# DPP attention stage: own-key products, value weights and the mask of the found places on GpSimd; values held for four tiles

## The chip, the core and the metric
The kernel runs on one core of a Trainium2 chip as one program. The core has five engines that each take instructions in their own order: PE (TensorE, matmuls), DVE (VectorE), ACT (ScalarE), POOL (GpSimd) and SP, which here only issues DMAs. They meet at semaphores alone. The metric is the device time of one execution in microseconds (us), and lower is better. Times below are of the profiled execution unless said otherwise.

## What is computed
Six layers follow one another on x of shape 32 x 16 x 16 x 192: a mamba layer, a Fourier layer, the attention of this case (`l2a`), a gated mixture of experts, a memory attention and a second mixture. The change touches the attention alone. It works on 32 images of 256 tokens (two tiles of 128), with 12 heads of 16 channels. For each query token it finds the 8 most similar earlier keys, forms all pairs and triples of the token itself with one or two of them, scores each by the log-determinant of its Gram matrix, and mixes the softmax outputs of these sets by the probabilities of the scores:

```python
sim = k @ q_i
sim = jnp.where(jnp.arange(Tn) <= i, sim, -jnp.inf)
_, top_idx = jax.lax.top_k(sim, M)                      # M = 8
...
for comb in COMBS:                                      # one or two of the 8 slots
    valid = slot_valid[slots].all(axis=1) & ~slot_is_i[slots].any(axis=1)
    idx = jnp.concatenate([jnp.full((nc, 1), i), top_idx[slots]], axis=1)
    K = k[idx]; V = v[idx]
    gram = jnp.einsum('cnd,cmd->cnm', K, K)
    log_det = jnp.log(jnp.where(valid, jnp.linalg.det(gram), 1.0) + 1e-06)
    w = jax.nn.softmax(jnp.einsum('cnd,d->cn', K, q_i) / HS ** 0.5, axis=1)
    out_s = jnp.einsum('cn,cnd->cd', w, V)
...
probs = jax.nn.softmax(scores / TEMP)
y_soft = probs @ outs
...
return y @ W_proj.T + b_proj
```

Places with an index of the token itself or later are void; that is the mask.

## The kernel before
`dpp_attention_phase` writes out one program per engine. An image has six steps `i` = 0 to 5 (STEPS). In a step the find works on four of the twelve heads (QUAD = 4) of one tile: `t = i // 3`, so steps 0 to 2 are tile 0, with 128 keys, and steps 3 to 5 tile 1, with 256. `steps` unrolls the first and the last image and runs the other 30 in a loop of two images; `back(lag)` names the step that lies `lag` steps behind, so each engine works on several steps at once. `q` counts steps, `r = n * 2 + t` counts tiles.

The path of one step's four heads:
- PE `scores` writes similarities into PSUM, one step ahead. DVE `find` takes four MAX8 (L2485) and four FIND_INDEX8 (L2489) from it, then masks with two small operations (L2498 into `gone`, L2501 into `idxm`).
- PE `turn_indices` turns `idxm` (L2622), ACT copies it to `idxT` (L2269), SP writes it to DRAM and reads it back spread over all partitions (`spread`).
- One step later DVE `compare` makes the one-hot (L2534) and PE `gather` fetches keys and values with it (L2660, 96 matmuls for tile 0, 192 for tile 1, into three PSUM buffers `g`). ACT copies them out to `keys` and `values` (L2261 to L2263).
- Two steps later DVE `products` multiplies keys with keys (L2514, L2516) and keys with the token's own key (L2519) into `prod`, and `sums` reduces all of it to `dots` (L2526).

The work for a whole tile follows at fixed lags behind its last step: `det_stage` (lag 3, in steps 2 and 5), `log_stage` (lag 4, steps 0 and 3), `weigh_stage` (lag 5, steps 1 and 4) and `add_out` (lag 6, steps 2 and 5). `weigh_stage` ends with the value weights: L2461 multiplies `values` with `alpha` into `pv`. In the same step PE `turn_output` sums and turns `pv` (L2632, 36 matmuls) into PSUM `m`, and ACT `turned` copies it to `yT` (L2241). In the next step PE `project` (L2642) runs right behind the scores, and DVE `add_out` (L2473) adds its result to `x_res` ahead of `compare`.

PE also computes the next image's projections in seven units (`front`), three in step 1 and two each in steps 2 and 3. POOL squares and splits the keys, 32 times four large operations, released by `prod_ready`, which DVE sets right before its reduction. Per step DVE's order is `find`, the tile stage, `add_out`, `compare`, `products`, `det_end`, `sums`; PE's is `turn_indices`, `scores`, `project`, `front`, `turn_output`, `gather`.

## Time and profile before

| | us |
|---|---|
| median of 3 runs | 6926.5 (6921.05 to 6927.41) |
| profiled execution | 6929.71 |
| its span, first to last instruction | 6928.0 |
| DVE busy in the span | 4586.2 |
| PE busy | 4892.4 |
| ACT busy | 2648.7 |
| POOL busy | 1447.6 |

The attention stage runs from about 1500 to 4590 us. In the page's slices one digit is a fortieth of the span, 173 us, in tenths of busy time. In a timeline a row gives start, duration, engine, line, operation and tiles; in square brackets stands the idle time before it and what ended it. A row with "x4" merges four instructions. The end of a matmul is modelled, so PE's durations are less sure than DVE's. L numbers of this section and of the rows are lines of the kernel before; in the changed kernel the same code stands up to 47 lines lower down.

### The profile page before, as it was taken

The numbers are of one execution on the slowest core, as the hardware profiler recorded it, in microseconds if no ns is written. First come the engines' busy times: TensorE is split into PE (matmuls) and PEld (weight loads), VectorE is DVE, ScalarE is ACT, GpSimd is POOL, SyncE is SP. The second block draws the span as 40 slices with busy tenths as digits, with TensorE's granted clock in tenths as the row PEclk, the third lists the DMA queues.
The fourth block names the chain that finished last, engine by engine and source line by source line (L and its number), as shares of the span: only waits on it lengthen the run. The fifth ranks groups of instructions, "written<-read, shape, count | busy, mean of one in ns | idle before, by whom it ended". The sixth has DMA issues, their size and how long they took to land. (4 is left out here: it accounts for less than half of the span.)

```text
span 6928.0 us, 139785 instructions
## 1 busy us (share of the span) xinstructions
PE 4892.4 (71%) x46024; PEld 3814.4 (55%) x46025; DVE 4586.2 (66%) x10128; ACT 2648.7 (38%) x8929; POOL 1447.6 (21%) x1237
## 2 busy tenths in 40 slices
PE   6777777967777777777777777751794397169990
PEld 2333335756656666666666566551583376169990
DVE  5777773249999999999999999952464444212223
ACT  3334332225555455554554555532220132223330
POOL 2332331110000000000000000005325300554447
PEclk8777778977676777667776676655897697589995
DMA  4000000011111111111111111111222102111113
GB/s 139 7 5 7 7 0 6 0 38 69 69 65 68 69 69 69 69 69 67 69 72 63 69 69 69 69 39 53 72 76 72 41 0 60 51 53 46 45 42 109
DMA packets 139932, 369.61 MB, mean 53 GB/s; under 512 B 29410, under 2 KB 94667, under 8 KB 113716
## 3 DMA queue, kind: packets, MB, share of 16 engines
q1 hardware_dynamic: 105556, 283.58, 11.8%
q0 software_dynamic: 33792, 78.69, 3.6%
q8 instruction: 313, 5.13, 0.3%
q14 instruction: 271, 2.22, 0.1%
HBM read 286.69 MB, written 75.50 MB: 52 GB/s over the span
## 5 line engine op out<-in xcount | busy, mean ns | idle before, releaser
L2660 PE MATMUL l2a_g<-l2a_feat,l2a_onehot 128*128 128x33 bf16 x27648 | 780.9, 183 | 403.7 <-ACT l2a_values L2263 202.1
L2660 PEld LDWEIGHTS l2a_g<-l2a_feat,l2a_onehot 128*128 128x128 bf16 x27648 | 765.3, 100 | 473.6 <-issue 237.3
L2526 DVE TENSOR_REDUCE l2a_dots<-l2a_prod 128x144 f32<-128x2304 f32 x192 | 489.6, 2550 | 4.5
L2609 PE MATMUL l2a_s<-l2a_qkT 32*128 32x128 f32 (+1 forms) x1536 | 486.1, 452 | 0.0
L1892 PE MATMUL l_y<-l_hc,l_selT 128*96 128x512 f32 x384 | 300.2, 876 | 262.2 <-POOL l_hc L1730 261.7
L2632 PE MATMUL l2a_m<-main_ident,l2a_pv 128*96 128x128 f32 x2304 | 335.2, 317 | 152.2 <-DVEq L2467 152.2
L2632 PEld LDWEIGHTS l2a_m<-main_ident,l2a_pv 128*96 128x96 f32 x2304 | 327.2, 199 | 172.3 <-issue 168.8
L1730 POOL TENSOR_TENSOR l_hc<-l_hs,l_bc 128x512 f32<-128x512 f32 x192 | 243.4, 1268 | 717.3 <-DVE l_hs L1797 716.1
L2534 DVE TENSOR_SCALAR l2a_onehot<-l2a_spread,l2a_pos 128x4096 bf16<-128x4096 bf16 x288 | 360.7, 1281 | 43.8 <-DVE l2a_hd L2428 20.1
L2609 PEld LDWEIGHTS l2a_s<-l2a_qkT 32*128 32x128 f32 x1536 | 310.6, 250 | 85.6 <-issue 37.9
L700 PE MATMUL l3f_expert_h<-l3f_tT,l3f_w_own 96*128 96x256 f32 x2592 | 333.6, 287 | 8.9 <-POOL l3f_w_own L657 6.7
L2514 DVE TENSOR_TENSOR l2a_prod<-l2a_keys 128x1536 f32<-128x1536 f32 x192 | 336.1, 1750 | 0.2 <-DVE l2a_pv L2465 0.2
L2304 POOL TENSOR_TENSOR l2a_rest_f<-l2a_feat 128x384 f32<-128x384 f32 x32 | 26.4, 826 | 1456.2 <-ACT l2a_feat L2173 1456.2
L764 DVE TENSOR_TENSOR l3f_tT<-l3f_expert_tp,l3f_tT 96x512 fp32r<-96x512 f32 x72 | 49.5, 687 | 421.5 <-ACT l3f_tT L731 421.5
L740 ACT ACTIVATE l3f_hT<-l3f_expert_h,l3f_b 128x256 f32<-128x256 f32 x432 | 181.0, 470 | 380.0 <-PE l3f_expert_h L700 380.0
L700 PEld LDWEIGHTS l3f_expert_h<-l3f_tT,l3f_w_own 96*128 96x128 f32 x2592 | 320.3, 191 | 9.5 <-issue 7.1
L2582 PE MATMUL l2a_a<-l2a_tT,l2a_wqk 96*96 96x256 f32 x768 | 309.9, 586 | 21.5 <-ACT l2a_tT L2160 21.5
L657 POOL TENSOR_TENSOR l3f_w_own<-l3f_w,l3f_w_own 96x1536 fp32r<-96x1536 f32 x72 | 252.9, 3514 | 326.0 <-DVE l3f_w_own L758 326.0
L715 PE MATMUL l3f_expert_y<-l3f_w,l3f_hT 128*128 x1728 | 292.6, 326 | 0.0
L1797 DVE TENSOR_TENSOR_SCAN l_hs<-l_dA,l_state,l_dBu 128x512 f32<-128x512 f32 x192 | 261.3, 1361 | 37.1 <-ACT l_dA L1680 28.7
L715 PEld LDWEIGHTS l3f_expert_y<-l3f_w,l3f_hT 128*128 128x128 f32 x1728 | 279.1, 190 | 0.0
L2261 ACT COPY l2a_keys<-l2a_g 128x128 f32<-128x128 f32 x768 | 202.7, 264 | 182.3 <-PE l2a_g L2660 167.7
(412 smaller groups left out, 11365.5 us busy)
## 6 DMA issues: line engine op xcount, KB each, us to landing
l2a_spread<-l2a_idx_rows SPq DMA_DIRECT2D x192, 1024.0 KB
rows_in<-main_zeros SPq DMA_DIRECT2D x1, 13824.0 KB, 59.6
l2f_xg<-rows_in SPq DMA_DIRECT2D x72, 192.0 KB, 2.4
rows_out<-l2f_ys POOLq DMA_DIRECT2D x72, 192.0 KB, 2.4
l3f_xg<-rows_in SPq DMA_DIRECT2D x72, 192.0 KB, 2.4
rows_out<-l3f_ys POOLq DMA_DIRECT2D x72, 192.0 KB, 2.4
...
```

The costliest lines, as they stand in the source:

```text
L657: nc.gpsimd.tensor_tensor(w1_own[:, u, 1, :, :], w1[:, :, bass.ds(e, 1), :].rearrange("p h a f -> p h (a f)"), w1_own[:, u, 0, :, :].bitca ...
L700: ins = nc.tensor.matmul(h_ps[b][:, c % 2, :], w1_own[:, u, wp, h, c * P:(c + 1) * P], tT[:, u, tp_, h, :], start=h == 0 and wp == tp_, st ...
L715: ins = nc.tensor.matmul(y_ps[u][:, t * C:(t + 1) * C], hT[:, u, c, t * P:(t + 1) * P], w2[:, c, bass.ds(e, 1), :].rearrange("p a c -> p ( ...
L1797: nc.vector.tensor_tensor_scan(hs[:, g % 2, :], dA[:, g % 2, :], dBu[:, g % 2, :], state[:, 0, g:g + 1], ALU.mult, ALU.add).then_inc(scan_ ...
L1892: nc.tensor.matmul(y_ps[:, :], selT[:, g, :], hc[:, g % 2, :], start=g == 0, stop=g == G - 1).then_inc(hc_used, 1)
L2514: nc.vector.tensor_tensor(every[:, :, SLOTS * HS:4 * SLOTS * HS].rearrange("p j (d x) -> p j d x", d=3), rows.unsqueeze(2).broadcast_to([P ...
L2526: nc.vector.tensor_reduce(dots[:, quad_of(s[2]), 0:NPROD], prod[:, :, :, :], AX.X, ALU.add).then_inc(S["dots_ready"], 1)
L2534: ins = nc.vector.tensor_scalar(onehot[:, kt, :], spread[:, :], pos[:, kt:kt + 1], None, ALU.is_equal)
L2582: ins = nc.tensor.matmul(o[0:HC, j * T:(j + 1) * T], wqk[:, h, 2 * (k - 1) + j, :], tT[0:HC, h, :], start=h == 0, stop=h == 1)
L2609: ins = nc.tensor.matmul(o, qkT[rows, u, j, t * P:(t + 1) * P], qkT[rows, u, 4 + j // 2, 0:nk], start=False, stop=j % 2 == 1, skip_group_c ...
L2632: ins = nc.tensor.matmul(m_ps[0:HC, h * P:(h + 1) * P], pv[:, a, h * HC:(h + 1) * HC], consts["ident"], start=a == 0, stop=a == SLOTS)
L2660: ins = nc.tensor.matmul(o[:, a * FEAT:a * FEAT + 2 * HS + 1], onehot[:, kt, at:at + P], feat3[:, s[1], kt, part, h, 0:2 * HS + 1], start= ...
```

## The change
The own-key product goes to POOL, into a buffer of its own of two halves (`cross_prod`), and DVE reduces twice, each into its part of `dots`. The value weights go to POOL in three pieces of four heads, in the step after `weigh_stage`, behind the new semaphore `calm`, which DVE raises when it comes to `sums`. The mask goes to POOL in three operations: the comparison into `away_mark`, a conversion of the indices to `idx_f`, and their sum into `idxm`; ACT fills `gone` from `away_mark`. `values` has four places instead of two. `turn_output` and `turned` move from lag 5 to lag 6, `project` into the middle of `gather`, `add_out` behind `sums`.

```diff
-        values = m.sb("values", [P, 2, H, SLOTS, HS + 1])
-        prod = m.sb("prod", [P, QUAD, NPROD, HS])
+        values = m.sb("values", [P, 4, H, SLOTS, HS + 1])
+        prod = m.sb("prod", [P, QUAD, NPROD - SLOTS, HS])
+        cross_prod = m.sb("cross_prod", [P, 2, QUAD, SLOTS, HS])
...
+                def mask_indices(n, u, i):
+                    q, t = count_of((n, u, i)), i // QUADS
+                    pool.wait_ge(S["scored"], counted(q * 2 + 2))
+                    pool.wait_ge(S["idx_found"], counted(q * 2 + 2))
+                    pool.wait_ge(S["idxT_psum"], counted(q))
...
+                    nc.gpsimd.tensor_scalar(out, idx[:, :, :], pos[:, t:t + 1], 1000.0, ALU.is_ge,
+                                            ALU.mult).then_inc(S["mask_chain"], 1)
+                    nc.gpsimd.tensor_scalar(idx_f[:, :, :], idx[:, :, :], 0.0, None, ALU.add
+                                            ).then_inc(S["mask_chain"], 1)
+                    pool.wait_ge(S["mask_chain"], q * 2 + 2)
...
+                    nc.gpsimd.tensor_tensor(idxm[:, :].rearrange("p (j a) -> p j a", j=QUAD), out, idx_f[:, :, :],
+                                            ALU.add).then_inc(S["idxm_ready"], 1)
+                def weigh_values(n, u, t):
+                    r = n * 2 + t
+                    pool.wait_ge(S["alpha_ready"], counted(r + 1))
+                    pool.wait_ge(S["yT_psum"], counted(r))
+                    for h in range(0, H, 4):
+                        ins = nc.gpsimd.tensor_tensor(
+                            pv[:, 0:SLOTS, h * HS:(h + 4) * HS].rearrange("p a (h d) -> p h a d", h=4),
+                            values[:, 2 * u + t, h:h + 4, :, 0:HS],
+                            alpha[:, h:h + 4, :].unsqueeze(3).broadcast_to([P, 4, SLOTS, HS]), ALU.mult)
+                    ins.then_inc(S["pv_ready"], 1)
+                def cross_products(s):
+                    q, t = count_of(s), s[2] // QUADS
+                    pool.wait_ge(S["kv_ready"], counted(q * QUAD + QUAD))
...
+                    nc.gpsimd.tensor_tensor(cross_prod[:, s[2] % 2, :, :, :], keys[:, s[2] % 2, :, 0:SLOTS, :],
+                                            mine.unsqueeze(2).broadcast_to([P, QUAD, SLOTS, HS]), ALU.mult
+                                            ).then_inc(S["cross_ready"], 1)
...
-                    s = back(3)
-                    if s and ((nxt and i == 4) or (i < 2 and in_range(n))):
-                        pool.wait_ge(S["prod_ready"], count_of(s) + 1)
+                    if back(3):
+                        pool.wait_ge(S["calm"], count_of(back(3)) + 1)
...
+                    if stage(back, OUT):
+                        weigh_values(*stage(back, OUT))
...
+                    if in_range(n):
+                        mask_indices(n, u, i)
+                    if back(2):
+                        cross_products(back(2))
...
                 def sums(s):
                     q = count_of(s)
+                    dve.sem_inc(S["calm"], 1)
                     dve.wait_ge(S["prod_ready"], q + 1)
-                    nc.vector.tensor_reduce(dots[:, quad_of(s[2]), 0:NPROD], prod[:, :, :, :], AX.X, ALU.add
-                                            ).then_inc(S["dots_ready"], 1)
+                    nc.vector.tensor_reduce(dots[:, quad_of(s[2]), SLOTS:NPROD], prod[:, :, :, :], AX.X, ALU.add)
+                    dve.wait_ge(S["cross_ready"], counted(q + 1))
+                    nc.vector.tensor_reduce(dots[:, quad_of(s[2]), 0:SLOTS], cross_prod[:, s[2] % 2, :, :, :], AX.X,
+                                            ALU.add).then_inc(S["dots_ready"], 1)
```

On DVE, at the end of step 2 (`l2a_ex` is the last result of `det_stage`, `main_x_res` that of `add_out`), before:

```order
L2403 TENSOR_TENSOR l2a_ex<-l2a_top,l2a_mx 128x12x32
L43 REGISTER_ALU
L2473 ISA [waits l2a_first_chain,l2a_proj_ready]
L2473 TENSOR_TENSOR main_x_res<-l2a_m,main_x_res 128x192
L2531 ISA
L2534 TENSOR_SCALAR l2a_onehot<-l2a_spread,l2a_pos 128x4096 [waits l2a_gathered,l2a_spread_in]
L2507 REGISTER_ALU
L2514 TENSOR_TENSOR l2a_prod<-l2a_keys 128x4x384 [waits l2a_kv_ready]
L2516 TENSOR_TENSOR l2a_prod<-l2a_keys 128x4x64
L2519 TENSOR_TENSOR l2a_prod<-l2a_keys,l2a_feat 128x4x128
L2411 TENSOR_TENSOR l2a_det<-l2a_both,l2a_bent 128x12x32 [waits l2a_squared]
L2526 TENSOR_REDUCE l2a_dots<-l2a_prod 128x4x36 [waits l2a_prod_ready]
```

and after:

```order
L2450 TENSOR_TENSOR l2a_ex<-l2a_top,l2a_mx 128x12x32
L43 REGISTER_ALU
L2566 ISA [waits l2a_first_chain]
L2569 TENSOR_SCALAR l2a_onehot<-l2a_spread,l2a_pos 128x4096 [waits l2a_gathered,l2a_spread_in]
L2543 REGISTER_ALU
L2550 TENSOR_TENSOR l2a_prod<-l2a_keys 128x4x384 [waits l2a_kv_ready]
L2552 TENSOR_TENSOR l2a_prod<-l2a_keys 128x4x64
L2458 TENSOR_TENSOR l2a_det<-l2a_both,l2a_bent 128x12x32 [waits l2a_squared]
L2559 TENSOR_REDUCE l2a_dots<-l2a_prod 128x4x28 [waits l2a_prod_ready]
L2561 TENSOR_REDUCE l2a_dots<-l2a_cross_prod 128x4x8 [waits l2a_cross_ready]
L2518 ISA [waits l2a_proj_ready]
L2518 TENSOR_TENSOR main_x_res<-l2a_m,main_x_res 128x192
```

The own-key product is gone, a second reduction waits for POOL, and `add_out` with its wait for the projection stands at the step's end.

On PE, in the same step 2, from the second pair of scores (`l2a_s`) on; `l2a_a` are the fronts, `l2a_g` the gather, `l2a_m<-l2a_wp` the projection. Before:

```order
L2604 MATMUL l2a_s<-l2a_mask_bf,l2a_ident_bf 128x2x128 [waits l2a_scored]
L2609 MATMUL l2a_s<-l2a_qkT 128x256 x2
L2642 MATMUL l2a_m<-l2a_wp,l2a_yT 128x192 [waits l2a_yT_ready,l2a_idxT_ready]
L2642 MATMUL l2a_m<-l2a_wp,l2a_yT 128x192
L2573 REGISTER_ALU
L2582 MATMUL l2a_a<-l2a_tT,l2a_wqk 96x256 [waits l2a_a_sb]
L2582 MATMUL l2a_a<-l2a_tT,l2a_wqk 96x256 x3
L2573 REGISTER_ALU
L2590 MATMUL l2a_a<-l2a_wtok,l2a_tT 128x384 [waits l2a_a_sb]
L2590 MATMUL l2a_a<-l2a_wtok,l2a_tT 128x384
L2653 ISA [waits l2a_onehot_ready]
L2660 MATMUL l2a_g<-l2a_feat,l2a_onehot 128x33 [waits l2a_kv_ready]
```

and after, from the output's turn (`l2a_pv`) on:

```order
L2665 MATMUL l2a_m<-main_ident,l2a_pv 96x128 x17
L2608 REGISTER_ALU
L2617 MATMUL l2a_a<-l2a_tT,l2a_wqk 96x256 [waits l2a_a_sb]
L2617 MATMUL l2a_a<-l2a_tT,l2a_wqk 96x256 x3
L2608 REGISTER_ALU
L2625 MATMUL l2a_a<-l2a_wtok,l2a_tT 128x384 [waits l2a_a_sb]
L2625 MATMUL l2a_a<-l2a_wtok,l2a_tT 128x384
L2688 ISA [waits l2a_onehot_ready]
L2695 MATMUL l2a_g<-l2a_feat,l2a_onehot 128x33 [waits l2a_kv_ready]
L2695 MATMUL l2a_g<-l2a_feat,l2a_onehot 128x33 x23
L2695 MATMUL l2a_g<-l2a_feat,l2a_onehot 128x33 [waits l2a_kv_ready]
L2695 MATMUL l2a_g<-l2a_feat,l2a_onehot 128x33 x23
```

The output's turn now stands ahead of the fronts, and the projection, which stood ahead of the fronts, comes only behind two quarters of the gather.

On POOL, in step 2, which was empty before, now stands:

```order
L2322 ISA [waits l2a_calm]
L2323 REGISTER_ALU [waits l2a_alpha_ready]
L2325 TENSOR_TENSOR l2a_pv<-l2a_values,l2a_alpha 128x4x8x16 [waits l2a_yT_psum]
L2325 TENSOR_TENSOR l2a_pv<-l2a_values,l2a_alpha 128x4x8x16 x2
L2306 ISA
L2308 REGISTER_ALU [waits l2a_idx_found,l2a_scored]
L2311 TENSOR_SCALAR l2a_away_mark<-l2a_idx,l2a_pos 128x4x8 [waits l2a_idxT_psum]
L2313 TENSOR_SCALAR l2a_idx_f<-l2a_idx 128x32
L2315 REGISTER_ALU
L2317 TENSOR_TENSOR l2a_idxm<-l2a_away_mark,l2a_idx_f 128x32 [waits l2a_mask_chain]
L2333 ISA
L2339 TENSOR_TENSOR l2a_cross_prod<-l2a_keys,l2a_feat 128x512 [waits l2a_kv_ready,l2a_dots_ready]
```

The value weights, the mask and the own-key product came here from DVE, in this order.

## Rows read from the trace of the kernel before

**Rows 1.** The page's slices of DVE, each digit a fortieth of the span.

```profile
DVE  5777773249999999999999999952464444212223
```

**Rows 2.** Stretches, one per step 0 to 5: bounds, length, busy us by engine, PEclk, DMA.

```profile
2911.64:2924.64 13.00, 7.71 (x165) 6.59 (x166) 12.36 (x26) 8.64 (x46) 0.00 (x0) 0.55 0.21 72
2924.64:2941.27 16.63, 14.94 (x155) 11.88 (x152) 15.73 (x37) 6.22 (x22) 1.74 (x1) 0.74 0.19 77
2941.27:2956.55 15.28, 14.88 (x203) 11.32 (x201) 14.44 (x38) 10.38 (x43) 0.00 (x0) 0.78 0.21 72
2956.55:2969.45 12.90, 9.90 (x46) 7.02 (x47) 12.21 (x26) 9.96 (x49) 0.00 (x0) 0.66 0.22 83
2969.45:2989.40 19.95, 15.32 (x265) 13.37 (x264) 19.04 (x41) 4.34 (x22) 1.87 (x3) 0.79 0.16 55
2989.40:3006.94 17.54, 9.86 (x238) 8.50 (x234) 16.71 (x39) 9.53 (x37) 1.81 (x1) 0.71 0.18 63
```

The busy columns are PE, PE's weight loads, DVE, ACT and POOL, each with its count.

**Rows 3.** Waits between engines, 1590 to 4410 us: total, times, longest.

```profile
PE l2a_m L2622 <- DVE l2a_idxm L2501: 119.6, 121, 2.3
...
DVE main_x_res L2473 <- PE l2a_m L2642: 1.3, 2, 0.7
```

**Rows 4.** Timeline of DVE in steps 1 and 2.

```profile
2932.14 1.75 DVE L2461 TENSOR_TENSOR l2a_pv<-l2a_values,l2a_alpha 128x1536 f32<-128x1536 f32 x1
...
2942.93 0.29 DVE L2489 FIND_INDEX8 l2a_idx<-l2a_top,l2a_s 128x8 uint32<-128x128 f32 x1
...
2943.73 0.25 DVE L2387 TENSOR_TENSOR l2a_cross_n<-l2a_dots,l2a_inv_own 128x96 f32<-128x96 f32 x1
...
2953.01 0.68 DVE L2519 TENSOR_TENSOR l2a_prod<-l2a_keys,l2a_feat 128x512 f32<-128x512 f32 x1
2953.61 0.55 DVE L2411 TENSOR_TENSOR l2a_det<-l2a_both,l2a_bent 128x384 f32<-128x384 f32 x1
```

**Rows 5.** Groups of POOL by line: count, busy us, mean ns, idle before.

```profile
L657 POOL TENSOR_TENSOR l3f_w_own<-l3f_w,l3f_w_own 96x1536 fp32r<-96x1536 f32 x72 | 252.9, 3514 | 326.0 <-DVE l3f_w_own L758 326.0
L1730 POOL TENSOR_TENSOR l_hc<-l_hs,l_bc 128x512 f32<-128x512 f32 x192 | 243.4, 1268 | 717.3 <-DVE l_hs L1797 716.1
```

**Rows 6.** Timeline of all engines in the mamba stage.

```profile
833.98 1.25 POOL L1722 TENSOR_TENSOR l_du_r<-l_du,l_du_r 96x512 fp32r<-96x512 f32 x1
834.06 2.26 DVE L1797 TENSOR_TENSOR_SCAN l_hs<-l_dA,l_state,l_dBu 128x512 f32<-128x512 f32 x1
```

**Rows 7.** Single lines: count, then shortest, median and longest in ns.

```profile
L1797 DVE TENSOR_TENSOR_SCAN l_hs<-l_dA,l_state,l_dBu x192: 1282/1284/2265, 52.1 to 1076.4; 128x512 f32<-128x512 f32 x192
L1832 DVE TENSOR_TENSOR l_sm<-l_sm x16: 161/1136/1141, 143.5 to 1086.4; 128x4 f32<-128x4 f32 x16
L2526 DVE TENSOR_REDUCE l2a_dots<-l2a_prod x192: 2542/2552/2555, 1530.7 to 4552.3; 128x144 f32<-128x2304 f32 x192
L2428 DVE TENSOR_REDUCE l2a_hd<-l2a_sc x64: 652/653/653, 1579.7 to 4568.6; 128x12 f32<-128x480 f32 x64
```

**Rows 8.** Timeline of PE, steps 1, 2 and 4.

```profile
2937.95 4.10 PE L2632 MATMUL l2a_m<-main_ident,l2a_pv 128*96 128x128 f32 x36
...
2944.38 0.23 PE L2622 MATMUL l2a_m<-l2a_ident_bf,l2a_idxm 128*32 128x128 bf16 x1
...
2947.08 1.65 PE L2642 MATMUL l2a_m<-l2a_wp,l2a_yT 96*128 96x192 f32 x4
2948.52 3.62 PE L2582 MATMUL l2a_a<-l2a_tT,l2a_wqk 96*96 96x256 f32 x8
...
2954.18 1.98 PE L2660 MATMUL l2a_g<-l2a_feat,l2a_onehot 128*128 128x33 bf16 x72
...
2980.38 6.19 PE L2632 MATMUL l2a_m<-main_ident,l2a_pv 128*96 128x128 f32 x36 [4.25 <-DVEq L2467]
```

**Rows 9.** Stretches of the fronts in step 2 and scores in step 3, columns as in rows 2.

```profile
2948.50:2954.20 5.70, 5.70 (x14) 3.40 (x13) 5.43 (x9) 4.36 (x16) 0.00 (x0) 0.53 0.39 122
2960.30:2965.00 4.70, 4.68 (x11) 2.62 (x11) 4.32 (x7) 3.75 (x18) 0.00 (x0) 0.54 0.01 3
```

More of the change, by code:

```diff
@@ L2271, in body @@
                             extend(n, u, i // QUADS)
+                    if stage(back, OUT):
+                        turned(*stage(back, OUT))
                     if stage(back, DET):
@@ L2286, in body @@
                             split_high(*nxt)
-                    if stage(back, WEIGH):
-                        turned(*stage(back, WEIGH))
                 for k in range(FRONT):
@@ L2434, in weigh_stage @@
                     r = n * 2 + t
-                    chain, link, send, tt = chained("third_chain", 17, r)
+                    chain, link, send, tt = chained("third_chain", 16, r)
                     TT = nc.vector.tensor_tensor
@@ L2543, in body @@
                             do(*stage(back, lag))
-                    if stage(back, OUT):
-                        add_out(*stage(back, OUT))
                     nxt = next_image(n, u, last)
@@ L2556, in body @@
                         sums(back(2))
+                    if stage(back, OUT):
+                        add_out(*stage(back, OUT))
                 own_facts(0, 0)
@@ L2644, in project, with gather @@
                     ins.then_inc(S["proj_ready"], 1)
-                def gather(s):
+                def gather(s, between):
                     q, t = count_of(s), s[2] // QUADS
@@ L2675, in body @@
                     if stage(back, OUT):
-                        project(*stage(back, OUT), held)
+                        turn_output(*stage(back, OUT), held)
                     if nxt:
@@ L2679, in body, with between @@
                             front(*nxt, k)
-                    if stage(back, WEIGH):
-                        turn_output(*stage(back, WEIGH), held)
+                    def between():
+                        if stage(back, OUT):
+                            project(*stage(back, OUT), held)
                     if back(1):
-                        gather(back(1))
+                        gather(back(1), between)
+                    else:
+                        between()
                 for k in range(FRONT):
```

62 lines of the change are left out of this document (29 added, 33 removed).

## Prediction

> **What bounds the kernel now.** I read the page's slices first: in the DPP stage DVE (VectorE) shows a 9 in nearly every one [rows 1]. Next come the busy times of one image, cut at the first MAX8 of each of its six steps. They last 13.00, 16.63, 15.28, 12.90, 19.95 and 17.54 us, together 95.30, and DVE works 12.36, 15.73, 14.44, 12.21, 19.04 and 16.71 us of them, 90.5 in all; GpSimd has 5.4 us of work [rows 2]. I call them steps 0 to 5 and write T for a step's first MAX8. The waits between engines: in 29.5 images DVE waits 1.3 us for PE's projection, PE 119.6 us for `idxm` [rows 3]. So DVE's own queue sets the end, and what leaves it is gained one for one, as long as nothing else holds DVE and nobody whom DVE waits for comes later. PE is second: in step 2 it works 14.88 of 15.28 us [rows 2]. Both conditions decide this case.
>
> **What leaves DVE, per image.**
> Own-key product (L2519): from its start at 2953.01 to the next one at 2953.61, 0.60 us [rows 4]; six times, 3.6 us.
> Value weights (L2461): 1.75 us [rows 4], twice, 3.5 us.
> Mask (L2498, L2501): in step 2 the last find starts at 2942.93, the first operation behind the mask at 2943.73 [rows 4]. A find of 0.29 us ends at 2943.22, and an operation with nothing to wait for starts 0.08 us before the end of the one ahead (2953.01 + 0.68 against 2953.61) [rows 4]; without the mask that would be 2943.14, 0.59 us earlier. Read in the same way the six steps give 0.59, 1.07, 0.59, 0.71, 0.90 and 0.59, sum 4.45 us; steps 1 and 4 are the dear ones, and GpSimd has work just there [rows 2].
> Added: the reduction is cut in two, over the same 2304 elements. 2304 take 2552 ns and 480 take 653 [rows 7]: 1.04 ns an element and 0.15 us fixed, of which some overlaps with the one before. I take 0.10 us, six times 0.6.
> DVE's queue gets shorter by 3.6 + 3.5 + 4.45 - 0.6 = 11.0 us, 350 us in 32 images, if nothing is given back.
>
> **What comes onto GpSimd, and what DVE pays for it.** No row has these operations there. The nearest is a TENSOR_TENSOR of 512 elements, 1268 ns; one of 1536 takes 3514 [rows 5]. So the own-key product is 1.27 us a step and the value weights 3 x 1.27 = 3.8 us twice an image. The two rows give 2.19 ns an element and 0.15 us fixed, 0.22 us for each of the three mask operations of 32 elements. Unknown is whether a comparison of integers costs more; the two bounds I keep are 0.15 and 0.5 us, and I take 0.23, 0.7 us a step.
>
> That time is not the price; the shared port is. In the mamba stage a DVE scan starts at 834.06, 0.08 us behind a GpSimd product that ends at 835.23, and takes 2.26 us [rows 6]; the median of its line is 1284 ns. L1832, a DVE operation with four elements, takes 161 ns at its shortest and 1136 in the median [rows 7], held for most of the 1.27 us of such a product. So a DVE operation with two operands in SBUF and a GpSimd operation run one after the other. The reduction L2526 however has 2542/2552/2555 ns in all 192 cases [rows 7], those with GpSimd's splits beside them too, and MAX8 and FIND_INDEX8 read PSUM. Hence:
> The value weights wait for `calm`, which DVE gives at its reductions; behind it lie 2.7 us of reductions and 2 us of MAX8 and finds. 3.8 us fit in: free.
> The mask comes right behind the finds, where DVE starts its det, log or weigh operations, nearly all with two operands. I charge its 0.7 us in full, since DVE has no gap there. `idxm`, ready some 0.5 us behind the last find today (2943.22, and 2943.73 for the operation behind the mask) [rows 4], then takes 1.2 us at least and 2.2 if each of the three waits for one DVE operation; I take 1.65.
> The own-key product follows the mask and needs ACT's copies of the keys, so it falls into the same operations: 1.2 us each; in step 0 the copies come so late that part of it meets a reduction and the gap behind: 0.5.
>
> The Trainium skill, SBUF, "Who interferes with whom", goes further than these rows: it says that the second of the two "fully blocks" for the rest of the first one's time, whichever of them came first, but only against a GpSimd operation that reads SBUF. All the moved ones do, so by it my charge would be a floor for each collision. Against the change as a whole speaks GPSIMD Engine Reference, "Engine selection": two-input elementwise work belongs on VectorE, with GpSimd about twice as slow. Twice the 0.68 us of L2519 [rows 4] would make the product an estimated 1.37 us, the image 0.5 us dearer; the row of 1268 ns is used.
>
> **Where DVE may have to wait.** The change moves the turn of the output (36 matmuls on `pv`) from step 1 into step 2, ahead of the fronts; the projection from ahead of the fronts into the middle of the gather; and DVE's `add_out` from the middle of step 2 to its end. DVE's own step 2 is 15.28 - 0.60 - 0.59 + 0.10 = 14.2 us, with the port's 1.9 it is 16.1; as `add_out` itself takes 0.6 of that with its wait, DVE gets there at T + 15.5.
> PE's path to the end of the projection: `idxm` at T + 1.95 + 1.65 = 3.6. Index turn and scores, 2944.38 to 2947.08: 2.7. The output's turn: 4.10 us behind a busy PE, 6.19 behind an idle stretch; PE is idle a short while only, so 4.1. The fronts, 2948.52 to 2954.18: 5.7. Half of the gather: 72 of its 96 matmuls take 1.98 us, so 1.3. The projection, 1.65 less its overlap: 1.4 [rows 8]. Sum: T + 18.8, with hand-over and `add_out` 19.3. The fronts shown ran at a granted clock of 0.53 [rows 9], nearly the lower level of 1.2 GHz throughout; an image in which half of them get the upper one saves 1.2 us, so I take T + 18.7 as the mean. Ends: T + 16.6 with all of it quick; T + 22 with the turn at 6.19 and the scores at the 4.7 us of step 3 [rows 9]. Step 2 gets longer by 3.4 us (1.3 to 6.7).
> Step 5 has the same new order but no fronts: `idxm` at T + 4.7, scores 2, turn 4.1 to 6.2; the gather starts with the one-hot near T + 13, so the projection ends near T + 17, DVE's reductions near T + 18. No wait. But on ACT `turned` now stands ahead of `bend` and the exponentials, which may push the logarithms that step 0 needs: 0.4 us, bounds 0 and 2.7. What else comes later I leave at nothing: the one-hot waits for index rows that come 1.1 us later in a step, and PE and ACT have that much slack in steps of over 13 us.
>
> **Sum per image.** Step 2: +3.4. The other five: own-key -3.0, mask -3.86, value weights -3.5, reduction +0.5, port for the mask 5 x 0.7 = +3.5, port for the product 0.5 + 4 x 1.2 = +5.3, late logarithms +0.4, together -0.7. In all +2.7 us, and 32 images make +86 us. The profiled execution took 6929.71 us with a span of 6928.0, 3 us above the median of 6926.5, which is nothing beside this; 6926.5 + 86 = **7012.5 us**.
>
> **The rivals.**
> A, the forecast: the port is paid nearly in full and DVE waits 2 to 5 us at `add_out` of step 2. Its own range is 6950 to 7075. Chance 0.42.
> B, the other side, faster: GpSimd's work slips into DVE's gaps. DVE is idle 4.8 of 95.3 us [rows 2], in small pieces between chained operations. With the port's 8.8 us in the five steps at a half, the image is 2.7 - 4.4 = -1.7 us: 6872. At a quarter 6802, at nothing 6731. It turns faster below 6.1 us of port an image. For it: no row shows a plain chain of short DVE operations against GpSimd. Against it: L1832 is short and was held nearly all the time. Chance 0.24, of which 0.05 below a quarter.
> C: PE is in time. If the projection ends before T + 15.5, step 2 is 16.1 us, +0.8, and the image +0.1: 6930, between 6890 and 6965. For it: 1.3 us of such waits today. Against it: step 2 has 14.88 us of PE work in 15.28 already. Chance 0.14.
> D: PE's slow end. With more idle stretches the granted clock stays at 0.54 as in step 3 [rows 9], step 2 ends at T + 22, the image is +6.7 - 0.7 = +6.0: 7118. Chance 0.15.
> E: neither port nor wait: 6926.5 - 350 = 6576. Chance 0.05.
>
> **How the numbers follow.** The predicted time is A's. The range of 6815 to 7120 leaves out E, the far part of B and half of D, 0.18. Cases of both signs hold much of the chance; A's own range stands above. Faster by over 0.2% (some 14 us, about what a measurement of this kernel can tell from no change): B 0.24, E 0.05, a third of C 0.04, so 0.33. Within 0.2%: half of C, 0.07. Slower: 0.60.
>
> **What would show it.** DVE's two-operand operations behind the finds get longer means than before, by 8 to 9 us an image in all, and GpSimd's own-key product has a median of 1.27 us or more. `add_out` waits about 3 us for PE's projection in step 2 and hardly in step 5. PE waits longer for `idxm`. The value weights lie inside reductions and finds. I am wrong if DVE's operations keep their times (B), if `add_out` never waits (C), or if a wait shows that I left at nothing: DVE at its second reduction for GpSimd's product, at the finds for `idxm`, at the one-hot for the index rows, or at the det for ACT's squares.

## The result, and the profile after

The changed kernel takes 7266.4 us (median of 4 runs, 7252.2 to 7268.0) against 6926.95 us of the kernel before beside it: a ratio of 1.0487, with a 95% interval of 1.0469 to 1.0506. That is 339.5 us more, 10.6 us an image where 2.7 were forecast, and above the range, which ended at 7120. The profiled execution has a span of 7250.6 us. L numbers from here on are lines of the kernel whose rows are shown.

The page's slices, to be read beside [rows 1]; the 9 of DVE has become an 8 through the whole stage, and GpSimd has gone from 0 to 3:

```profile
DVE  5777772268888888888888888883166434212223
...
POOL 2233321123333333333333333320622600354446
```

Five steps of the changed kernel, columns as in [rows 2]; they are steps 0, 1, 2, 4 and 5:

```profile
2948.72:2963.67 14.95, 9.14 (x220) 8.03 (x221) 13.33 (x24) 14.12 (x66) 5.76 (x6) 0.66 0.19 71
2963.67:2979.83 16.16, 12.46 (x145) 9.25 (x142) 15.32 (x34) 5.32 (x20) 9.23 (x8) 0.68 0.20 69
2979.83:3000.51 20.68, 17.37 (x162) 13.94 (x158) 14.62 (x36) 7.21 (x32) 2.66 (x4) 0.75 0.14 52
2908.41:2929.94 21.53, 14.41 (x305) 11.26 (x303) 20.76 (x38) 5.80 (x29) 11.76 (x10) 0.69 0.13 51
2929.94:2948.72 18.78, 13.62 (x195) 12.42 (x195) 16.78 (x36) 5.12 (x22) 2.66 (x4) 0.73 0.16 58
```

In step 2 DVE works 14.62 of 20.68 us, against 14.44 of 15.28 before. One image is not typical in every step, so here is the mean distance between the first MAX8s of successive steps over 31 or 32 images (us), read off DVE's timeline. Three kernels of the experiments stand beside it:

| step | 0 | 1 | 2 | 3 | 4 | 5 | sum |
|---|---|---|---|---|---|---|---|
| before | 12.95 | 16.41 | 15.29 | 12.75 | 19.82 | 17.89 | 95.11 |
| after | 14.59 | 16.82 | 20.29 | 12.74 | 21.45 | 19.99 | 105.88 |
| e8, move alone | 13.86 | 16.88 | 18.22 | 12.71 | 20.27 | 18.41 | 100.34 |
| e9, three mends | 13.35 | 14.37 | 17.44 | 11.64 | 17.64 | 19.47 | 93.92 |
| c3, fastest | 11.81 | 15.49 | 14.17 | 11.76 | 19.62 | 17.26 | 90.10 |

Step 2 brings 5.0 of the 10.8 us, step 5 2.1, steps 0 and 4 1.6 each.

Waits between engines, 1590 to 4700 us, columns as in [rows 3] (`l2a_det` is `det_end`, `main_x_res` is `add_out`):

```profile
PE l2a_m L2655 <- POOL l2a_idxm L2317: 364.9, 117, 5.9
PE l2a_g L2695 <- ACT l2a_values L2266: 309.2, 72, 6.8
DVE l2a_det L2458 <- ACT l2a_bent L2202: 172.1, 59, 4.9
DVE main_x_res L2518 <- PE l2a_m L2675: 24.3, 29, 0.8
```

The wait that was forecast, at `add_out`, is small. DVE waits 172 us at a place where it never waited before: `det_end`, for ACT's `bend`. The timeline of step 2 (first MAX8 at 2979.83) shows the chain behind it, first PE, then ACT, then DVE:

```profile
2983.81 0.29 PE L2655 MATMUL l2a_m<-l2a_ident_bf,l2a_idxm 128*32 128x128 bf16 x1 [3.31 <-POOL l2a_idxm L2317]
2984.35 2.07 PE L2644 MATMUL l2a_s<-l2a_qkT 32*128 32x256 f32 x4
...
2988.68 6.43 PE L2665 MATMUL l2a_m<-main_ident,l2a_pv 128*96 128x128 f32 x36
2994.95 1.89 PE L2617 MATMUL l2a_a<-l2a_tT,l2a_wqk 96*96 96x256 f32 x8
...
2999.18 0.90 PE L2675 MATMUL l2a_m<-l2a_wp,l2a_yT 96*128 96x192 f32 x4
```

```profile
2995.15 0.37 ACT L2246 COPY l2a_yT<-l2a_m 96x256 f32<-96x256 f32 x1 [10.24 <-PE l2a_m L2665]
...
2995.76 0.52 ACT L2202 ACTIVATE l2a_bent<-l2a_bent 128x384 f32<-128x384 f32 x1
```

```profile
2983.79 1.16 DVE L2441 COPY l2a_away<-l2a_away 128x48 f32<-128x48 f32 x1
...
2991.38 0.42 DVE L2552 TENSOR_TENSOR l2a_prod<-l2a_keys 128x256 f32<-128x256 f32 x1
2996.32 0.56 DVE L2458 TENSOR_TENSOR l2a_det<-l2a_both,l2a_bent 128x384 f32<-128x384 f32 x1 [4.51 <-ACT l2a_bent L2202]
```

`bend`, whose inputs were complete at 2984.95, when the copy of `l2a_away` ended, stands in ACT's order behind `turned`, and `turned` waits 10.24 us for PE's turn of the output. So DVE stands still for 4.51 us. The stretches of that chain (scores, turn, fronts), columns as in [rows 2]:

```profile
2983.80:2988.68 4.88, 4.87 (x12) 2.64 (x12) 4.38 (x10) 0.69 (x4) 1.10 (x1) 0.50 0.01 2
2988.68:2994.95 6.27, 6.27 (x38) 6.27 (x38) 3.12 (x3) 0.00 (x0) 0.00 (x0) 0.63 0.45 167
2994.95:2997.97 3.02, 3.02 (x15) 2.00 (x13) 1.66 (x2) 2.82 (x13) 0.00 (x0) 1.00 0.02 5
```

The granted clock had been 1.00 in the gather just before PE's idle 3.31 us. Behind them it was 0.50, the lower level, for the scores, which took 4.88 us instead of the 2.7 of the sum, and 0.63 in the mean of the turn, 6.3 us instead of 4.1. The upper level came back within the turn's last 2.45 us (0.83 there), and the fronts had it throughout.

The second surprise is in steps 1 and 4. GpSimd, then DVE, in step 1, whose MAX8 is at 2963.67:

```profile
2972.70 5.48 POOL L2325 TENSOR_TENSOR l2a_pv<-l2a_values,l2a_alpha 128x512 f32<-128x512 f32 x3 [3.64 <-DVEq L2557]
```

```profile
2973.46 2.61 DVE L2550 TENSOR_TENSOR l2a_prod<-l2a_keys 128x1536 f32<-128x1536 f32 x1
2975.99 1.27 DVE L2552 TENSOR_TENSOR l2a_prod<-l2a_keys 128x256 f32<-128x256 f32 x1
2977.30 2.02 DVE L2559 TENSOR_REDUCE l2a_dots<-l2a_prod 128x112 f32<-128x1792 f32 x1
```

"DVEq L2557" is DVE's sequencer (the part that reads the program and hands work to the engine) at the line that raises `calm`. In the program it stands between the products and the reduction; in time it came 4.6 us before the reduction, as an instruction of its own with no data to work on. The Trainium skill, Perfetto Trace Analysis, "Sequencer Loop", describes this order: the sequencer pushes engine instructions into a queue, where they wait for their semaphores, and starts executing a control instruction itself. The trace agrees with it. So the value weights ran beside DVE's products, and both paid: the products took 2.61 and 1.27 us, 1.75 and 0.42 undisturbed, and GpSimd's three pieces 5.48.

The price behind the finds was 187 us over 31 images: by so much DVE's operations outside the products, one-hots, finds and reductions became longer, 6.0 us an image, where 8 to 9 had been forecast. The own-key product has a median of 1.19 us, below the 1.27 of the forecast's sign. GpSimd's groups, columns as in [rows 5]:

```profile
L2325 POOL TENSOR_TENSOR l2a_pv<-l2a_values,l2a_alpha 128x512 f32<-128x512 f32 x192 | 358.2, 1891 | 226.7 <-DVEq L2557 200.2 <-DVEq L2512 26.5
L2339 POOL TENSOR_TENSOR l2a_cross_prod<-l2a_keys,l2a_feat 128x512 f32<-128x512 f32 x192 | 267.5, 1393 | 174.5 <-DVEq L2557 117.3 <-ACT l2a_values L2266 55.7
L2311 POOL TENSOR_SCALAR l2a_away_mark<-l2a_idx,l2a_pos 128x32 f32<-128x32 uint32 x192 | 121.5, 633 | 989.1 <-DVE l2a_idx L2535 989.0
L2313 POOL TENSOR_SCALAR l2a_idx_f<-l2a_idx 128x32 f32<-128x32 uint32 x192 | 92.3, 481 | 0.0
L2317 POOL TENSOR_TENSOR l2a_idxm<-l2a_away_mark,l2a_idx_f 128x32 bf16<-128x32 f32 x192 | 79.1, 412 | 35.2 <-POOL l2a_idx_f L2313 35.2
```

### The profile page after: what moved, and what is told of

The parts are those of the page before. It is cut to its first block and busy times, and to the rows that moved or that the text cites. A ratio compares the mean times of both kernels' runs of the same rounds, so it can differ in the third digit from the quotient of the medians.

```text
span 7250.6 us, 142196 instructions
## 1 busy us (share of the span) xinstructions
PE 4996.6 (69%) x46024; PEld 3893.6 (54%) x46025; DVE 4673.8 (64%) x9680; ACT 2632.3 (36%) x8993; POOL 2378.5 (33%) x2197
## 5 line engine op out<-in xcount | busy, mean ns | idle before, releaser
L2644 PE MATMUL l2a_s<-l2a_qkT 32*128 32x128 f32 (+1 forms) x1536 | 611.1, 548 | 0.0
L2569 DVE TENSOR_SCALAR l2a_onehot<-l2a_spread,l2a_pos 128x4096 bf16<-128x4096 bf16 x288 | 429.9, 1521 | 69.1 <-PE l2a_g L2695 28.7
L2644 PEld LDWEIGHTS l2a_s<-l2a_qkT 32*128 32x128 f32 x1536 | 387.2, 308 | 115.6 <-issue 76.5
L2311 POOL TENSOR_SCALAR l2a_away_mark<-l2a_idx,l2a_pos 128x32 f32<-128x32 uint32 x192 | 121.5, 633 | 989.1 <-DVE l2a_idx L2535 989.0
L2325 POOL TENSOR_TENSOR l2a_pv<-l2a_values,l2a_alpha 128x512 f32<-128x512 f32 x192 | 358.2, 1891 | 226.7 <-DVEq L2557 200.2
L2665 PE MATMUL l2a_m<-main_ident,l2a_pv 128*96 128x128 f32 x2304 | 404.4, 358 | 32.0 <-POOL l2a_pv L2325 31.6
L2550 DVE TENSOR_TENSOR l2a_prod<-l2a_keys 128x1536 f32<-128x1536 f32 x192 | 421.1, 2193 | 0.2 <-DVE l2a_pv L2510 0.2
L2559 DVE TENSOR_REDUCE l2a_dots<-l2a_prod 128x112 f32<-128x1792 f32 x192 | 387.3, 2017 | 4.5
L2339 POOL TENSOR_TENSOR l2a_cross_prod<-l2a_keys,l2a_feat 128x512 f32<-128x512 f32 x192 | 267.5, 1393 | 174.5 <-DVEq L2557 117.3
L445 POOL DMA_INDIRECT rows_in<-l3f_dispatch_xn,l3f_dispatch_at x128 | 122.9, 960 | 536.2 <-ACT l3f_dispatch_xn L421 497.5
```

What stands on the lines that cost most here:

```text
L2325: ins = nc.gpsimd.tensor_tensor(pv[:, 0:SLOTS, h * HS:(h + 4) * HS].rearrange("p a (h d) -> p h a d", h=4), values[:, 2 * u + t, h:h + 4, ...
L2339: nc.gpsimd.tensor_tensor(cross_prod[:, s[2] % 2, :, :, :], keys[:, s[2] % 2, :, 0:SLOTS, :], mine.unsqueeze(2).broadcast_to([P, QUAD, SLO ...
L2550: nc.vector.tensor_tensor(every[:, :, 0:3 * SLOTS * HS].rearrange("p j (d x) -> p j d x", d=3), rows.unsqueeze(2).broadcast_to([P, QUAD, 3 ...
L2559: nc.vector.tensor_reduce(dots[:, quad_of(s[2]), SLOTS:NPROD], prod[:, :, :, :], AX.X, ALU.add)
L2569: ins = nc.vector.tensor_scalar(onehot[:, kt, :], spread[:, :], pos[:, kt:kt + 1], None, ALU.is_equal)
L2644: ins = nc.tensor.matmul(o, qkT[rows, u, j, t * P:(t + 1) * P], qkT[rows, u, 4 + j // 2, 0:nk], start=False, stop=j % 2 == 1, skip_group_c ...
```

## The experiments

The theory after the two traces was that three losses add up: a late chain on PE and ACT, the value weights at the wrong time, and the port behind the finds. The rival: one of them is the cause and the others are its shadows. Each expectation numbers its own theories. First the waits were mended in the changed kernel, and parts of the change made alone in the kernel before. The kernel before ran again beside each group of experiments, with medians from 6918.8 to 6927.1 us; a ratio goes by the median beside it, and a difference in us between kernels of different groups can be off by some 8 us.

**e1: `turned` behind `bend` on ACT.**

```diff
-                    if stage(back, OUT):
-                        turned(*stage(back, OUT))
                     if stage(back, DET):
                         bend(*stage(back, DET))
+                    if stage(back, OUT):
+                        turned(*stage(back, OUT))
+                    if stage(back, DET):
                         logs(*stage(back, DET))
```

> The changed kernel with one order changed on ACT: in steps 2 and 5 `bend` (whose squares DVE's `det_end` waits for) comes ahead of `turned` again, which waits for PE's turn of the output. In the changed kernel DVE stands 180 us in all before the det (line 2458) for ACT, 4.5 us of it in step 2 and 1.3 in step 5 of the image read. Theory 1, the wait is the cost by itself: the 180 us go, 7266 becomes about 7085. Theory 2, the wait only hides the next one: the projection ends at T + 20.3 in step 2 whatever ACT does, so DVE stands before `add_out` instead; only step 5 gains its 1.3 us and the logarithms come some earlier in steps 0 and 3: 7266 - 32 x 2 = about 7200, and the idle time before `main_x_res` rises from 36 us to over 130.

7196.8 us, ratio to before 1.0398 (1.0380 to 1.0415). The groups of DVE:

```profile
L2459 DVE TENSOR_TENSOR l2a_det<-l2a_both,l2a_bent 128x384 f32<-128x384 f32 x64 | 35.4, 553 | 0.2 <-DVE l2a_ex L2451 0.2
L2519 DVE TENSOR_TENSOR main_x_res<-l2a_m,main_x_res 128x192 f32 (+1 forms) x64 | 22.9, 357 | 171.1 <-PE l2a_m L2676 171.1
```

The 180 us at `det_end` are gone, and 135 of them are back at `add_out`, as in theory 2: on average it waits 4.4 us in step 2 and 1.0 in step 5. The first wait hid the one that was forecast.

**e2: GpSimd released by DVE's last product (`prod_ready`, raised by the product itself) instead of `calm`.**

```diff
-                        pool.wait_ge(S["calm"], count_of(back(3)) + 1)
+                        pool.wait_ge(S["prod_ready"], count_of(back(3)) + 1)
```

> The changed kernel with GpSimd's large work (value weights, squares, splits) released by `prod_ready`, which DVE's last product raises when it is finished, instead of `calm`, a semaphore instruction in DVE's queue. In the trace of the changed kernel `calm` comes 4.6 us ahead of the reduction (value weights start at 2972.70, the reduction at 2977.30), and the value weights take 5.5 and 6.6 us beside one-hot and products, which are longer by 1.7 us in step 1 and 2.5 in step 4. Theory 1 (early release costs DVE those): 4.2 us an image, 7266 - 134 = about 7130, products back at means of 1.75 and 0.42 us except where the own-key product meets them, value weights near 1.2 us a piece. Theory 2 (the value weights only cost wherever they are, since they now push the mask and `idxm` later in steps 2 and 5): under 40 us gained, 7225 or more.

7074.4 us, ratio 1.0223 (1.0206 to 1.0240): one line gains 192 us, more than the 134 of theory 1. The weights now take 1056 ns each, not 1891:

```profile
L2325 POOL TENSOR_TENSOR l2a_pv<-l2a_values,l2a_alpha 128x512 f32<-128x512 f32 x192 | 197.6, 1056 | 469.9 <-DVE l2a_prod L2552 443.7 <-DVEq L2512 26.2
```

DVE's products lose 94 us, its one-hots 38, and `det_end` waits 56 us less.

**e4: the kernel before with the mask alone on GpSimd** (as in the change; `add_out` where it was).

> The kernel before with the mask alone on GpSimd (three operations, ACT fills `gone` from them); own-key products, value weights and all orders as before. In the changed kernel the three take 0.63, 0.48 and 0.42 us in the mean and `idxm` is ready 1.9 to 2.7 us behind the last find instead of 0.5. Theory 1 (port): DVE loses 4.45 us of its own an image and gets back 0.6 to 1.0 us a step by held operations, so -0.5 to +1.5 us an image: 6910 to 6975. Theory 2 (late indices): PE starts scores, fronts and gather 1.5 to 2 us later in each step, and steps 1 and 2, where PE is nearly full, get longer by it: 3 us or more an image, 7020 or more, with DVE waiting for keys, scores or the projection. Theory 3 (the mask was the good part): 4.45 us gained, 6785.

6911.5 us, ratio 0.9987 (0.9977 to 0.9996). 127 us leave DVE, and other operations get only some 50 us longer, 0.25 us a step. Most of the rest goes into waits; in step 2 `add_out` now waits for the projection:

```profile
2560.17 0.36 DVE L2495 TENSOR_TENSOR main_x_res<-l2a_m,main_x_res 128x192 f32 x1 [2.33 <-PE l2a_m L2655]
```

**e5: the kernel before with the own-key product alone on GpSimd**, behind ACT's copies of the keys.

> The kernel before with the own-key product alone on GpSimd and the reduction cut in two; GpSimd takes it as soon as ACT's copies of the keys are there, with no mask ahead of it. DVE saves 3.6 us an image and pays 0.85 for the second reduction (102 us less and 130 more in the changed kernel). Theory 1 (port, exclusive): each product holds a two-operand or one-hot operation for 1.0 to 1.2 us, unless it falls under finds or a reduction, which I expect for two of six: +4.4 - 2.75 = +1.6 us an image, about 6980. Theory 2 (the port costs little when the product comes alone): 6840. Theory 3 (all six collide): 7060.

6971.9 us, ratio 1.0071 (1.0054 to 1.0088). 131 us of product leave, the split of the reduction costs 28, and some 150 come onto what the product collides with, 0.9 us on average in each step but step 0; this line, 558 ns before, has a mean of 971:

```profile
L2438 DVE TENSOR_TENSOR l2a_z<-l2a_z,l2a_ex 128x384 f32<-128x384 f32 x64 | 62.1, 971 | 2.2
```

**e6: the value weights and the moved output, without the other two parts; e8: the same with the weights back on DVE; e11: e8 with e1's mend.** The weights' part of the edit that e8 takes back:

```diff
-                    if stage(back, OUT):
-                        weigh_values(*stage(back, OUT))
...
+                    link(TT(pv[:, 0:SLOTS, :].rearrange("p a (h d) -> p h a d", h=H), values[:, 2 * u + t, :, :, 0:HS],
+                            alpha[:, :, :].unsqueeze(3).broadcast_to([P, H, SLOTS, HS]), ALU.mult))
```

> The kernel before with one part of the change: value weights on GpSimd behind `calm`, four places for values, and with them the output's turn, `turned`, projection and `add_out` at their new places. Own-key product and mask stay on DVE. Mask alone gave 6911.5 us and the own-key product alone 6971.9, against 6922.3 for the kernel before, +39 together, where the whole change gives +344. Theory 1, this part carries the loss by itself: the weights stretch DVE's one-hot and products of steps 1 and 4 by some 4.2 us an image and save 3.5, and det_end waits for the output's turn, a little less than in the changed kernel since DVE's mask gives the indices to PE earlier: 7100 us (7050 to 7170), with a wait of DVE's det for ACT's bend of 2 us or more in step 2. Theory 2, only the three together lose, because the late indices of GpSimd's mask push PE's path: 6960 us (6930 to 7000) and a det wait under 1 us.

> The kernel of the run e6_values_alone with the value weights back on DVE in weigh_stage: nothing has gone to GpSimd, only the output's turn and `turned` stand a step later, the projection in the middle of the gather and add_out behind the sums (and GpSimd's squares and splits wait for `calm`). e6 gave +265 us over the kernel before. Theory 1, the larger part of that is the move: DVE's det waits for ACT's bend behind `turned`, about 95 us, and some 60 us of one-hot and add_out waits: 7060 us (7020 to 7090). Theory 2, it is GpSimd's value weights stretching DVE's operations and the move costs little by itself: 6950 us (6920 to 6980).

> e8_move_alone with bend ahead of turned. e8 lost 165 us with nothing on GpSimd. If the wait at det (58 us) only hid the wait for the projection, as in e1: 7065 us (7050 to 7080), with add_out waiting 60 us or more in the trace. If bend's place was all of it and the rest is the later work behind it on ACT (exponentials, logs): 7010 (6990 to 7030).

e6 took 7184.1 us (ratio 1.0385, 1.0364 to 1.0406), above even the first theory's range, e8 7084.4 (1.0238, 1.0217 to 1.0258), e11 7075.2 (1.0215, 1.0194 to 1.0235). With nothing new on GpSimd the move of the output costs 165 us. In e8 DVE waits 122 us longer, 58 of them at `det_end` and 10 more than before at `add_out`:

```profile
L2411 DVE TENSOR_TENSOR l2a_det<-l2a_both,l2a_bent 128x384 f32<-128x384 f32 x64 | 35.5, 554 | 58.1 <-ACT l2a_bent L2201 57.9 <-DVE l2a_ex L2403 0.2
L2473 DVE TENSOR_TENSOR main_x_res<-l2a_m,main_x_res 128x192 f32 (+1 forms) x64 | 22.5, 352 | 35.7 <-PE l2a_m L2641 35.7
```

and in e11 at `add_out` alone, for nearly the same time:

```profile
L2474 DVE TENSOR_TENSOR main_x_res<-l2a_m,main_x_res 128x192 f32 (+1 forms) x64 | 22.7, 354 | 98.9 <-PE l2a_m L2642 98.9
```

So the place of `turned` on ACT only names another waiter. The other 36 us of e8 are DVE operations that take longer, this one above all, 658 ns before:

```profile
L2445 DVE TENSOR_TENSOR l2a_ex<-l2a_ex,l2a_z 128x480 f32<-128x480 f32 x64 | 67.9, 1060 | 2.2
```

GpSimd's old squares and splits hold them: ACT's copies, for which they wait, come later, so that the second split, where it falls into step 1, starts on average 2.85 us behind the first MAX8 instead of 0.63, and the squares of step 4 3.6 us instead of 1.8. e8 also lets GpSimd wait for `calm`, but the idle time before its squares and splits ends with ACT's copies. The turn, the projection and `add_out` were moved together in e8, and no run takes them apart.

e6 minus e8: 112 us leave DVE with the weights, and the kernel is 100 us slower; the products (+134), the one-hot (+25) and `det_end` (+37) show it. The values part together carries 265 of the 340 us, theory 1 of e6.

**e3: e1 and e2 together; e7: the same on e6; e9: e3 with the own-key product at the head of GpSimd's step; e10: e9 with front unit 4 in step 3 instead of 2.** The edits of e9 and e10:

```diff
                         pool.wait_ge(S["prod_ready"], count_of(back(3)) + 1)
                         hold(pool, S["pool_held"])
+                        cross_products(back(3))
...
-                    if back(2):
-                        cross_products(back(2))
...
-        UNITS = {1: (0, 1, 2), 2: (3, 4), 3: (5, 6)}
+        UNITS = {1: (0, 1, 2), 2: (3,), 3: (4, 5, 6)}
```

> The changed kernel with both mends, e1 (bend ahead of turned on ACT, -70 us) and e2 (GpSimd released by DVE's last product, -192 us). If the two losses are independent, 7266 - 262 = 7004 us (6985 to 7025). If both are waits for the same late chain on PE (indices, scores, turn, fronts, projection), the second mend brings only part: 7050 (7030 to 7070).

> The kernel of the run e6_values_alone with both mends of e1 and e2: `turned` behind `bend` on ACT, and GpSimd released by DVE's last product instead of `calm`. Stretched products and one-hots (some 160 us in e6) should go to a fifth, the det wait (95 us) should go and half of it come back as a wait for the projection: 7184 - 130 - 50 = 7000 us (6970 to 7030). If it ends below 6919, the value weights would pay once they are released rightly; I expect not, because the output's turn stands in step 2, where PE is full.

> The changed kernel with three mends: bend ahead of turned (e1), GpSimd released by DVE's last product (e2), and the own-key product at the head of GpSimd's step, so that it runs beside DVE's first reduction and not behind the mask. In c1 that third one was worth 130 us against e5. If that price is independent of the rest: 7032 - 130 = 6902 us (6880 to 6925). If the remaining waits (projection, indices) hide part of it, or the value weights are pushed 1.3 us out of their window by the product ahead of them: 6970 (6940 to 7000).

> e9_three_mends with front unit 4 moved from step 2 to step 3. What is left of the loss should be the wait of add_out for the projection in step 2, which stands behind the fronts. If so, 1.8 to 2.3 us of the 4 us wait go in each image, less what the unit costs in step 3: 50 us faster than e9 (35 to 70). If the wait is set by something else (indices, turn), less than 15 us.

e3: 7031.8 us (1.0162, 1.0142 to 1.0182), between the two forecasts: of 262 us 235 came, so the two losses are mostly independent. e7: 6955.5 (1.0052, 1.0034 to 1.0070), below its range: the weights, rightly released, now gain, but less than the move costs. e9: 6884.3 (0.9934, 0.9918 to 0.9951), some 150 us faster than e3 and now faster than before. e10: 6861.5 (0.9906, 0.9889 to 0.9922), only 23 us faster than e9, where 35 to 70 were expected. The `away` copy of 48 elements and `add_out`, in e9:

```profile
L2518 DVE TENSOR_TENSOR main_x_res<-l2a_m,main_x_res 128x192 f32 (+1 forms) x64 | 22.9, 358 | 158.4 <-PE l2a_m L2675 158.4
L2441 DVE COPY l2a_away<-l2a_away 128x48 f32<-128x48 f32 x64 | 12.1, 189 | 9.3 <-DVE l2a_bent L2439 0.2
```

The copy, 929 ns on average in e3, is back to 189, and the one-hots lose 54 us: the collisions with the own-key product are over. What is left is above all the wait for the projection, on average 3.1 us in step 2 and 1.9 in step 5. In e10 it falls to 121 us; some 15 of those 37 us come back elsewhere.

**The candidates, built up from the kernel before.** c1 moves the own-key product alone, at the head of GpSimd's step and released by `prod_ready`; c2 adds the mask and puts `add_out` behind the sums, with the projection still right behind the scores; c3 adds e10's line; c4 adds the value weights of tile 1 alone, with their turn and projection in step 5.

> The kernel before with the own-key product on GpSimd, released by DVE's other products of the same step, so that it runs while DVE is in the first of the two reductions; value weights, mask and output as before. Theory 1, a reduction does not feel GpSimd, only the two-input operations do: the price of the run with the own-key product behind the finds (150 us on held operations) goes, and -131 for the product and +28 for the second reduction are left: 6820 us (6800 to 6845). Theory 2, what GpSimd does then it does at the cost of something else (its squares and splits of steps 4, 0 and 1 start 1.4 us later and so meet DVE's chains, and the second reduction waits for the product): 6870 (6850 to 6910).

> The kernel of the run c1_key_in_sums with also the mask on GpSimd, and add_out behind the sums at the step's end (the projection stays right behind the scores). Theory 1: the mask leaves DVE (-127 us), its port costs 45 to 50, and the 98 us of waiting for the projection that it brought alone are gone because add_out now stands 8 us later: c1 - 80, 6740 us (6720 to 6770). Theory 2, PE's queue is the bound of step 2 (it worked 14.88 of 15.28 us), so the later indices come back as a wait of DVE for gathered keys or for the scores of step 3: c1 - 15, 6805 (6775 to 6830).

> The kernel of the run c2_mask_too with one of the two front units of step 2 (number 4) moved to step 3, on PE and ACT. If PE's queue bounds step 2 (theory 2 of the run c2_mask_too), step 2 loses 1.8 to 2 us of PE work in front of its gather and the kernel gains up to 60 us over c2; if DVE bounds it (theory 1), it is the same as c2 within 10 us, or slower by up to 20 because step 3's gather then waits.

> The kernel of the run c3_fronts_later with the value weights of tile 1 alone on GpSimd, in the reduction and the finds that follow step 4, right behind the own-key product; their turn, projection and add_out stand in step 5, where PE works 9.9 of 17.5 us, and `turned` behind bend and the exponentials. Tile 0 stays as before, since its turn would come into step 2. Theory 1: 1.75 us x 32 = 56 us leave DVE, the 3.8 to 4.5 us of weights behind 1.3 us of product run about 1 us past the finds into DVE's step 5 chain, 0.5 to 1 us given back: 6730 us (6710 to 6750). Theory 2, what overruns holds DVE's det chain and what ACT and PE do later in step 5 makes the logs or the gather late: 6775 (6755 to 6800).

c1: 6842.0 us (0.9890, 0.9873 to 0.9906). The product beside the reduction, in c1's timeline:

```profile
2959.45 2.01 DVE L2536 TENSOR_REDUCE l2a_dots<-l2a_prod 128x112 f32<-128x1792 f32 x1
2959.50 1.19 POOL L2310 TENSOR_TENSOR l2a_cross_prod<-l2a_keys,l2a_feat 128x512 f32<-128x512 f32 x1 [15.44 <-DVE l2a_prod L2530]
...
2961.38 0.67 DVE L2538 TENSOR_REDUCE l2a_dots<-l2a_cross_prod 128x32 f32<-128x512 f32 x1
```

Neither feels the other, and the second reduction never waits. Against e5 only the product's place and release differ, and they are worth 130 us. c2: 6772.3 (0.9788, 0.9772 to 0.9805), 70 us more gained, nearer to the first forecast than to the second. A wait of DVE at the logarithms, 2.6 us in all in c1, is new in it:

```profile
L2460 DVE SCALAR_TENSOR_TENSOR l2a_sc<-l2a_sc,l2a_veto 128x96 f32<-128x96 f32 x64 | 16.7, 262 | 30.4 <-ACT l2a_sc L2224 30.4
```

c3: **6755.9 us** (0.9765, 0.9748 to 0.9781), the fastest: 163 us below the kernel before, some 510 below the changed one. Against c2 it gains 16 us: that wait falls to 4.7 us, and some of it comes back elsewhere. c4: 6813.1 (0.9844, 0.9828 to 0.9861), 57 us slower than c3 and slower than both its forecasts; the wait comes back as soon as one turn is moved, 1.9 us in step 5:

```profile
L2528 DVE TENSOR_TENSOR main_x_res<-l2a_m,main_x_res 128x192 f32 (+1 forms) x64 | 22.5, 352 | 63.1 <-PE l2a_m L2686 63.1
```

In c3 the same line is idle for 8 us.

**Who held DVE.** In each trace, over 31 images, I took every DVE operation that was over 0.1 us longer than the median of its kind in the kernel before, and put the excess down to the GpSimd operation that it overlapped longest (us):

| GpSimd operation | before | after | e2 | e5 | e4 | e9 |
|---|---|---|---|---|---|---|
| own-key product | | 178 | 178 | 149 | | 0 |
| value weights | | 131 | 0 | | | 4 |
| mask, three operations | | 0 | 0 | | 0.4 | 0.1 |
| squares and splits (not moved) | 11 | 68 | 68 | 1 | 43 | 69 |

The mask's operations hold practically nobody. What e4 pays stands in steps 1 and 4, beside the squares and splits, which start later there (in step 4 3.7 us behind the first MAX8 instead of 1.8).

## Why the prediction was wrong

The direction was right, the size was a quarter of the real one. The forecast's own terms, put together by parts and compared with the runs, in us per image (the time difference divided by 32):

| part | forecast | run | measured |
|---|---|---|---|
| output moved | +2.65 | e8 - before | +5.2 |
| value weights | -3.5 | e6 - e8 | +3.1 |
| own-key product | +2.8 | e5 - before | +1.5 |
| mask | +0.8 | e4 - before | -0.3 |
| all together, beyond the sum | 0 | | +1.1 |

The forecasts are its sums: step 2 without the mask's 1.15 us of delay, 2.25, and the logarithms 0.4; weights -3.5; -3.0 + 0.5 + 5.3; -3.86 + 3.5 + 1.15. The errors have both signs; two are large, and both make the kernel slower.

**The step that failed** is the sentence that the value weights wait for `calm`, "which DVE gives at its reductions", and so are free. I took the place of an instruction in the program for its place in time. The weights came 4.6 us earlier and cost nearly twice what they saved: an error of 6.6 of the 7.9 us. e2 and e7 show it: released by the product itself, the weights gain what was forecast (e11 to e7, which also undoes the early release: -112 us, each against the kernel before beside it, -3.5 us an image).

**The second** is the move. The sum followed PE to the projection and let DVE arrive at `add_out`; it saw that `turned`, which waits for that turn, stands ahead of `bend` on ACT, and charged 0.4 us for late logarithms, but that this holds `det_end` was left at nothing and named only among the signs of being wrong. e1 shows that this by itself is worth 70 us and no more, because the projection is late as well. There the terms were mis-sized: scores 4.9 us for 2.7, turn 6.3 for 4.1, the indices at T + 4.0 for T + 3.6, less 2.7 for quicker fronts; the projection ended at T + 20.3 instead of 18.8. Both rows for the slow values stood in [rows 8] and [rows 9], and I chose the quick one for the turn because "PE is idle a short while only"; it was idle for 3.3 us, and the granted clock was 0.50 behind that. They are the values of rival D, which had a chance of 0.15 and ended at 7118 us. Step 5, "No wait", got 2.1 us longer, with a mean wait of 1.6 us at `det_end`. And the sum left at nothing what the move does to GpSimd's old squares and splits, 36 us in e8.

**Right, with the wrong size.** The port: the product behind the finds costs 4.7 us an image in e5 and 5.6 in the changed kernel, for the 6.5 charged over six steps. The mask's three operations take 0.63, 0.48 and 0.41 us instead of 0.23 each, yet hold practically none of DVE's; the 0.25 us a step that e4 shows instead of 0.7 are held by squares and splits. For the mask's operations the mechanism was wrong, and why they hold so little is not settled by any run. The Trainium skill, SBUF, "Who interferes with whom", has a DVE instruction with two SBUF inputs contend with any GpSimd instruction that reads SBUF; e4 doesn't bear that out for these small operations. The same section also lists copies and tensor-scalar operations as able to take the shared pair of ports; I had charged two-operand operations only. Here the traces agree with it; in the changed kernel the one-hot, 1281 ns before, and the `away` copy, 188 ns before, have these groups:

```profile
L2569 DVE TENSOR_SCALAR l2a_onehot<-l2a_spread,l2a_pos 128x4096 bf16<-128x4096 bf16 x288 | 429.9, 1521 | 69.1 <-PE l2a_g L2695 28.7 <-DVE l2a_ex L2450 19.0 <-DVE l2a_pv L2510 9.8
...
L2441 DVE COPY l2a_away<-l2a_away 128x48 f32<-128x48 f32 x64 | 73.1, 1142 | 9.3 <-DVE l2a_bent L2439 0.2
```

**Right** was the reduction, which takes 2.01 or 2.02 us with GpSimd beside it. The split costs less than the 0.6 us an image that were forecast: the durations grow by 0.86, but neighbours overlap, and from the start of the sums to the start of what follows it is 2.53 us for 2.47 in a step, 0.36 an image.

What stays open is the 1.1 us an image beyond the sum of the parts, and why e10's gain stops short of its forecast. e3's 235 of 262 us speak for waits that share one late chain on PE, but no run isolates it.
